# The batch loop of an adaLN attention and expert kernel, written over its 24 score units instead of over 16 steps

## The reference, cut to what matters

```python
h = _layernorm(x) * (1 + ca) + sa
Q, K, V = split_heads(h @ W_q.T), split_heads(h @ W_k.T), split_heads(h @ W_v.T)   # 16 heads of 2*8
A1 = causal(einsum(Q1, K1) * scaling);  A2 = causal(einsum(Q2, K2) * scaling)
O = (softmax(A1) - lam * softmax(A2)) @ V
O = O / sqrt(mean(O * O, -1) + EPS) * rms_scale * (1.0 - LAMBDA_INIT)
x = x + ga * (O @ W_o.T)
h = _layernorm(x) * (1 + cb) + sb
logits = h @ router_w.T + router_b          # top 2 of 8, softmax over the two
x = x + gb * sum over the two experts of gate * (silu(h @ gate_w.T) * (h @ up_w.T)) @ down_w.T
```

## Time and profile before

| | |
|---|---|
| median of 3 runs | 1679.91 us (1677.23 to 1682.1) |
| the profiled execution | 1678.91 us, span 1677.1 us |
| PE busy | 1340.8 us, 80% of the span |
| DVE busy | 1228.7 us, 73% |
| ACT busy, POOL busy | 859.4 us, 857.3 us, 51% each |
| mean granted clock of TensorE | 0.903 of 2.4 GHz |

### The profile page before, as it was taken

How to read it: one execution, slowest core, us unless ns; L and a number is a source line. 1 busy time by engine, 2 the same in 40 slices (tenths; PEclk the granted TensorE clock), 3 DMA queues, 4 the chain that set the end, 5 groups by cost and what they waited for, 6 DMA issues and landing times. The chain is left out here.

```text
span 1677.1 us, 44178 instructions
## 1 busy us (share of the span) xinstructions
PE 1340.8 (80%) x14048; PEld 940.4 (56%) x14049; DVE 1228.7 (73%) x3090; ACT 859.4 (51%) x1918; POOL 857.3 (51%) x1283
## 2 busy tenths in 40 slices
PE   1578888888888888888888888885199999999960
PEld 0345555555555555555555555553178888888850
DVE  3467887888888888888888888876756666666647
ACT  1156667666766676667666766664123333333320
POOL 0135566666666666666666666665323333333334
PEclk9999989998999899989998999896589999999985
DMA  5453444344434443444344434410111111111129
GB/s 203 99 111 76 112 109 101 86 111 109 105 85 108 112 105 84 111 111 105 83 111 111 106 83 108 105 39 17 43 44 44 44 44 46 43 44 45 44 76 296
DMA packets 182624, 151.73 MB, mean 90 GB/s; under 512 B 29555, under 2 KB 165369, under 8 KB 182068
## 3 DMA queue, kind: packets, MB, share of 16 engines
q1 hardware_dynamic: 165124, 122.11, 30.2%
q0 software_dynamic: 8448, 16.93, 3.3%
q10 hardware_dynamic: 8880, 10.49, 1.8%
HBM read 88.26 MB, written 60.51 MB: 89 GB/s over the span
## 5 line engine op out<-in xcount | busy, mean ns | idle before, releaser
L1190 DVE TENSOR_REDUCE mx<-p_max 128x2 f32<-128x512 f32 (+1 forms) x768 | 504.9, 685 | 198.3 <-PE p_max L816 188.9
L1009 ACT ACTIVATE probs<-p_exp 128x512 f32<-128x512 f32 x768 | 440.4, 601 | 239.7 <-PE p_exp L837 150.9
L1430 POOL TENSOR_SCALAR_AFFINE_SELECT probs<-probs 128x256 f32<-128x256 f32 (+1 forms) x768 | 366.3, 486 | 344.6 <-ACT probs L1009 333.3
L866 PE MATMUL p_out<-probs,v 128*32 128x256 f32 (+1 forms) x4096 | 253.3, 371 | 42.1 <-ACT ot L1000 35.7
L659 POOL DMA_INDIRECT pair_out<-on,v x136 | 133.7, 983 | 282.4 <-ACT on L569 274.6
L808 PE MATMUL p_max<-kt,qt 50*128 50x256 bf16 x1024 | 199.3, 293 | 35.6 <-ACT probs L1009 19.0
L866 PEld LDWEIGHTS p_out<-probs,v 128*32 128x32 f32 x4096 | 124.0, 119 | 145.2 <-POOL probs L1430 67.9
L837 PE MATMUL p_exp<-qt,kt 52*128 52x256 bf16 x1024 | 205.2, 289 | 0.0
L816 PE MATMUL p_max<-tri,ids 64*128 64x128 bf16 (+1 forms) x768 | 188.7, 253 | 0.0
L633 DVE TENSOR_TENSOR ot<-ot,p_max 128x512 f32<-128x512 f32 x136 | 93.5, 688 | 123.6 <-PE p_max L520 105.0
L816 PE MATMUL p_max<-tri,idb 64*128 64x128 bf16 (+1 forms) x768 | 172.3, 252 | 0.0
(11 more groups left out here) (174 smaller groups left out, 2750.5 us busy)
## 6 DMA issues: line engine op xcount, KB each, us to landing
qt<-q_parts SPq DMA_DIRECT2D x128, 192.0 KB
q_parts<-part_h SPq DMA_DIRECT2D x96, 128.0 KB, 1.9
kt<-k_parts SPq DMA_DIRECT2D x128, 96.0 KB
v<-rows_sorted SPq DMA_DIRECT2D x136, 65.0 KB, 1.8
q_parts<-part_m SPq DMA_DIRECT2D x64, 128.0 KB, 1.9
kt<-k_parts SPq DMA_DIRECT2D x128, 64.0 KB
qt<-pair_out SPq DMA_DIRECT2D x32, 256.0 KB, 5.0
mods<-mod_rows SPq DMA_DIRECT2D x32, 192.0 KB
```

The source lines that it names most:

```text
L866: m = nc.tensor.matmul(p_out[32 * j:32 * j + 32, pair, SEQ - n:SEQ], v[:, b.par, tile, 2 * g + head, :], src, start=(tile == 0), stop=(til ...
L1009: nc.scalar.activation(probs[:, quad % 2, k, :], p_exp[:, n % 3, :], ACT.Exp, scale=SCALE).then_inc(exp_done.sem, 1)
L1190: V.reduce_max(mx[:, w, tile, t, heads[0]:heads[-1] + 1], p_max[:, bank, :].rearrange("p (h k) -> p h k", h=len(heads)), AX.X, negate=True ...
L1430: G.affine_select(out=blocks, in_=blocks, compare_op=ALU.is_ge, fill=zero, base=0, pattern=[[0, count], [1, P]], channel_multiplier=-1).th ...
```

## The change

The loop `for s in range(16)` becomes `for u in range(24)` on PE, DVE, ACT and POOL. Each engine does one unit and then the extra work that the code names for that u. No product, reduce or copy is added or left out, and all sizes stay. What changes is after which unit each extra piece stands (units counted from 0; before, an even step s stands after unit s + s // 2, an odd one after the second of its two units, and a number with a star is a piece that DVE does between the two units of an odd step):

| piece | engine | after unit, before | now |
|---|---|---|---|
| `outputs` 6, 7 of bC | PE | 0, 3 | 0, 2 |
| `outputs` 0 to 5 of b2 | PE | 6, 9, 12, 15, 18, 21 | 6, 8, 12, 14, 18, 20 |
| `xn` transposes, `project` 0, `project` 1 | PE | 0, 2, 5 | 3, 4, 7 |
| `on_tok` transposes, `wo`, `h2` transposes | PE | 3, 5, 6 | 3, 5, 7 |
| `outputs_to_rows` of bC | PE | 8, 9 | 10, 11 |
| logits, V product, ranks | PE | 11, 12, 15 | 9, 13, 16 |
| `max_to_rows` of b2, of b1 | PE | 2, 14 | 1, 14 |
| `outputs_to_rows` of b2 | PE | 20, 21 | 17, 19 |
| `on_tok`, `xtmp` | DVE | 0, 6 | 1, 7 |
| `rest_part` 0, 1 | DVE | 3, 6 | 6, 9 |
| first statistics, their means | DVE | 7*, 9 | 2, 3 |
| `normalise` of bC | DVE | 9, 10* | 11, 13 |
| `minus_max` of b2, of b1 | DVE | 0, 12 | 0, 12 |
| top 8; indices and `topf`; `chosen`, `both` | DVE | 13*, 13*, 13* | 11, 14, 15 |
| second statistics, their means | DVE | 12, 13* | 15, 16 |
| sum of squares; ranks and carry; positions | DVE | 16*, 16*, 18 | 17, 18, 20 |
| `normalise` of b2 | DVE | 21, 22* | 19, 21 |
| `inverse_roots` 1 and 2, 3 and 4 | DVE | 21, 21 | 22, 23 |
| `copy_outputs` 3 of bC, 0 to 2 of b2 | ACT | 5, 11, 17, 23 | 3, 9, 15, 21 |
| `xn`, `h2` of the next turn's batches | ACT | 23 | 0, 1 of that turn |
| scatter of four row tiles (indirect DMA) | POOL | 18, 20, 21, 23 | 21, 22, 22, 23 |
| `o` = sum of two halves, `osq` = its square | POOL | 12, 14 | 14, 15 |

The two `outputs_to_rows` of bC also change banks, and the lists `MISC0` and `MISC1` with them. The diff, cut to its core:

```diff
-        MISC0 = [(ht_ready, 1, 2), (r_ready, 1, 2), (r_ready, 2, 2), (on2_ready, 4, -1),
+        MISC0 = [(ht_ready, 1, 2), (r_ready, 1, 2), (r_ready, 2, 2), (on2_ready, 3, -1),
                  (v_ready, 1, 1), (on2_ready, 1, 0)]
         MISC1 = [(nmt_ready, 2, 0), (ont_ready, 1, -2), (attn_scaled, 1, -2), (h2t_ready, 1, -3),
-                 (on2_ready, 3, -1), (route, 1, -3), (nmt_ready, 1, 1), (route, ROUTE_CARRY, -3),
+                 (route, 1, -3), (on2_ready, 4, -1), (nmt_ready, 1, 1), (route, ROUTE_CARRY, -3),
...
-                for s in range(NH):
-                    n = s + s // 2
-                    scores(b1, b2, n)
-                    if s % 2:
-                        scores(b1, b2, n + 1)
-                    if s % 2 == 0:
-                        g = s // 2 - 2
-                        if g >= 0 and active(b2):
-                            outputs(b2, g)
-                        if g < 0 and active(bC):
-                            outputs(bC, g + PAIRS)
-                    if s == 0 and active(bA):
-                        mix_free(pe, i, 0, 0)
-                        wait(pe, xn_ready, bA)
-                        for tile in range(NT):
-                            m = nc.tensor.transpose(p_mix[:, 0, tile * P:(tile + 1) * P], xn[:, tile, :], idf[:])
-                        m.then_inc(xt_ps.sem, 1)
...
+                    scores(b1, b2, u)
+                    if u in (0, 2) and active(bC):
+                        outputs(bC, PAIRS - 2 + u // 2)
+                    if u in (6, 8, 12, 14, 18, 20) and active(b2):
+                        outputs(b2, 2 * (u // 6 - 1) + u % 6 // 2)
+                    if u == 1 and active(b2):
                         max_to_rows(i, b2, 1, 0)
...
+                    if u == 3 and active(bA):
...
+                    if u == 4 and active(bA):
                         wait(pe, ht_ready, bA)
                         project(i, bA, 0, 1)
...
+                    if u == 5 and active(bW):
...
-                    if s == 3 and active(bA):
-                        project(i, bA, 1, 2)
-                    if s == 5 and active(bC):
-                        outputs_to_rows(i, bC, 1, 0, 1, 4)
-                    if s == 6 and active(bC):
-                        outputs_to_rows(i, bC, 1, 1, 0, 3)
-                    if s == 4 and active(bR):
+                    if u == 7 and active(bR):
                         mix_free(pe, i, 1, 3)
...
-                    if s == 7 and active(bR):
-                        mix_free(pe, i, 1, 5)
+                    if u == 7 and active(bA):
+                        project(i, bA, 1, 2)
+                    if u == 9 and active(bR):
+                        mix_free(pe, i, 1, 4)
                         wait(pe, h2t_ready, bR)
...
+                    if u == 10 and active(bC):
+                        outputs_to_rows(i, bC, 1, 0, 0, 3)
+                    if u == 11 and active(bC):
+                        outputs_to_rows(i, bC, 1, 1, 1, 5)
...
-                    if s == 9 and active(b1):
+                    if u == 14 and active(b1):
                         max_to_rows(i, b1, 0, 6)
-                    if s == 10 and active(bR):
+                    if u == 16 and active(bR):
 
...
-                    if s == 13 and active(b2):
+                    if u == 17 and active(b2):
                         outputs_to_rows(i, b2, 0, 0, 0, 5)
-                    if s == 14 and active(b2):
+                    if u == 19 and active(b2):
                         outputs_to_rows(i, b2, 0, 1, 1, 8)
 
...
-                    if s == 15 and (active(bL) or active(bW)):
-
...
+                    if u == 0 and (active(bA) or active(bR)):
+
+                        act.wait_ge(newton, NEWTON * (i.n + LEAD - 1))
+                    if u == 0 and active(bA):
...
+                    if u == 2 and active(bL):
+                        wait_half(dve, x_loaded[bL.par], bL)
...
+                    if u == 6 and active(bA):
                         rest_part(bA, 0)
-                    if s == 4 and active(bW):
+                    if u == 7 and active(bW):
...
-                    if s == 4 and active(bA):
+                    if u == 9 and active(bA):
                         rest_part(bA, 1)
...
+                    if u == 10 and active(bR):
+
...
+                    if u == 11:
                         for k in range(2):
                             if active(bC):
...
-                    if s == 7 and active(bC):
...
+                    if u == 12 and active(b1):
+                        minus_max(b1, 0, 0)
...
+                    if u == 13 and active(bC):
                         for k in range(2):
-                            normalise(bC, 1, 1, 0, k)
...
-                            V.tensor_tensor(lg[:], p_mix[:, 1, 0:NT * NE].rearrange("p (t e) -> p t e", t=NT),
-                                            rb[:].unsqueeze(1).to_broadcast([P, NT, NE]), ALU.add).then_inc(route.sem, 1)
-                        if active(bW):
-                            wait(dve, x1_ready, bW)
-                            settle(dve)
...
+                    if u == 14:
                         if active(bR):
                             wait(dve, route, bR, ROUTE_TOP)
...
+                    if u == 15:
+                        if active(bR):
                             wait(dve, route, bR, 6)
                             V.tensor_tensor(chosen[:], iota8[:].unsqueeze(1).to_broadcast([P, 2 * NT, NE]),
                                             topf[:].rearrange("p j t -> p (j t)").unsqueeze(2).to_broadcast([P, 2 * NT, NE]),
                                             ALU.is_equal).then_inc(route.sem, 1)
+                        if active(bW):
+                            wait(dve, x1_ready, bW)
+                            settle(dve)
+                            statistics(bW, 1, stats2)
+                        if active(bR):
                             wait(dve, route, bR, 7)
                             V.tensor_tensor(both[:], chosen[:, 0:NT, :], chosen[:, NT:2 * NT, :], ALU.add).then_inc(route.sem, 1)
-                    if s == 11 and active(bC):
+                    if u == 16 and active(bW):
+                        for tile in range(NT):
+                            mean_and_variance(bW, 1, stats2, tile)
+                    if u == 17 and active(bC):
                         wait(dve, osq_ready, bC)
                         V.reduce_sum(rms_ss[:], osq[:], AX.X).then_inc(rms_sum.sem, 1)
-                    if s == 11:
+                    if u == 18:
...
-                    if s == 14:
-                        if active(b2):
-                            for k in range(2):
-                                normalise(b2, 0, 0, 0, k)
-                        inverse_roots(i, [1, 2, 3, 4])
...
+                    if u == 22:
+                        inverse_roots(i, [1, 2])
+                    if u == 23:
+                        inverse_roots(i, [3, 4])
...
-                    if s in (12, 13, 14, 15) and active(bR):
-
-                        k = s - 12
+                    for k in {21: (0,), 22: (1, 2), 23: (3,)}.get(u, ()):
```

More of the change, by code:

```diff
@@ L1095, in body @@
-                    if s == 15 and active(bW):
-                        if not (bW.static and bW.c < 2):
-                            wait_half(act, scattered[bW.par], bW.plus(-2))
-                        wait(act, h2t_ps, bW.plus(-2))
-                        wait(act, h2_copied, bW.plus(-2))
-                        settle(act)
-                        for tile in range(NT):
-                            c = NT * NH + NT + tile
-                            nc.scalar.activation(h2[:, bW.par, 0, tile, 0:DIM], xres[:, bass.ds(bW.n * SEQ + tile * DIM, DIM)],
-                                                 ACT.Identity, bias=neg_mr[:, NT + tile:NT + tile + 1],
-                                                 scale=rstd[:, c:c + 1]).then_inc(xn2_ready.sem, 1)
@@ L1439, in body @@
                 bA, b2, bC, bW, bR = (i.plus(d) for d in (2, 0, -1, -2, -3))
-                for s in range(NH):
+                for u in range(NBANKS):
                     if active(b2):
-                        mask_bank(b2, s + s // 2)
-                        if s % 2:
-                            mask_bank(b2, s + s // 2 + 1)
-                    if s == 5 and active(bW):
-                        wait(pool, attn_scaled, bW)
-                        xb = xres[:, bass.ds(bW.n * SEQ, SEQ)]
-                        G.tensor_tensor(xb, xb, xtmp[:].rearrange("p t c -> p (t c)"), ALU.add).then_inc(x1_ready.sem, 1)
-                    if s in (4, 6) and active(bA):
-                        low_part(bA, (s - 4) // 2)
-                    if s == 0 and active(bR):
+                        mask_bank(b2, u)
+                    if u == 2 and active(bR):
                         wait(pool, xn2_ready, bR)
@@ L1459, in body @@
```

(8 more changed lines are left out.)

182 lines of the change are left out of this document (92 added, 90 removed).

## The result

The changed kernel takes **1837.85 us** (median of 4 runs, 1831.29 to 1842.33), the kernel before 1681.01 in the same session (4 runs, 1677.23 to 1684.34): a ratio of **1.093, interval 1.089 to 1.098**, 9.3% slower. The forecast was 1722, its range ended at 1775. The direction was right, the size a quarter of what came. The profiled execution takes 1831.29 us (span 1829.5), 152.4 more than that of before.

A forecast was written before the change was run, and what follows sets the result against it. PE was taken to bound units 0 to 7 and DVE the rest. Larger parts 31.7 plus waits gave 33.6, plus clock 1.4 made 35.0 us a turn against 33.6: 1722 us over 31 turns, range 1645 to 1775.

The forecast's parts named there:

- the sum of the larger parts: Over seven ranges of units, the larger of PE's and DVE's work adds up to 31.7 us a turn.
- the waits and the walk: Per-range work of 31.7 plus waits of 1.1, 0.5 and 0.3: 33.6 us a turn, against 32.0 for the old turn.
- the price of the clock: Cost of PE's clock falling at units 15 and 16 and slowing 17 to 20: 1.4 us a turn, 1.6 before.
- `xtmp`: PE's h2 transposes behind unit 7 wait for DVE's xtmp, with nothing covering it: 1.1 us a turn.
- `both`: PE idles 2.4 us after unit 16, before the ranks, waiting for DVE's both; it was 1.12.
- `ht`: PE's project 0 waits for ACT's ht with only unit 4 between: 0.5 us a turn.
- `rest_part` 1: PE's outputs_to_rows of bC waits for it at unit 10: 0.2 us a turn.
- The rival of the free POOL: DVE's minus_max, topf and chosen no longer blocked by POOL: 32.8 us a turn, 1654 us; chance of faster 0.28.
- The three savings in the rival's sum: DVE's minus_max, topf and chosen save 1.1, 0.4 and 0.7 us, 2.2 in all, where DVE bounds the turn.
- What the other moves bring lies under cover.: Other moves, such as earlier copy_outputs and POOL's scatters, change nothing because DVE's list is full in those units.
- the clock as one fall per turn: A fall at units 15 and 16 costs from nothing to 3.3 us a turn; 1.4 was taken.
- The lead-in at nothing: Lead-in and tail cost nothing, having the same turns and chain; any one edit there would show some 3 us.

The follow-up runs named there:

- early_split: The changed kernel with the chain that makes Q's and K's parts moved back to about where it stood before: 1766.29 us, ratio 1.052.
- es_route: early_split with DVE's indices and topf after unit 12, chosen after 13 and both after 14: 1797.09 us, ratio 1.073.
- late_low: The kernel before with only POOL's second low_part moved from after unit 9 to after unit 12: 1713.89 us, ratio 1.019.
- split_saves: The changed kernel with SP's Q saves waiting for low_part 0 alone and only the K saves for low_part 1: 1797.35 us, ratio 1.071.
- load_first: The changed kernel with SP's loads for unit 0 issued ahead of move_max instead of behind it: 1806.45 us, ratio 1.077.
- es_xtmp: early_split with DVE's xtmp after unit 6 instead of after unit 7: 1736.22 us, ratio 1.032.

## Why the prediction was right and wrong

**Right in the main: the sum of the larger parts.** PE sets the pace of some units and DVE of others, and the change moved work so that both lists are full at different places. early_split, in which the loop is nearly idle (12.5 us of weight loads' waits for `kt` between 200 and 1200 us), has turns of 35.21 and 36.47 us in a row, mean 35.74; the forecast was 35.0. In its terms: the waits and the walk were to add 1.6 us a turn (33.6 against 32.0), and PE's idle time grew by 2.3; the price of the clock was to fall by 0.2 (1.4 against 1.6), and PE's busy time fell by 0.15. That the sum holds range by range of units was not measured. (Its seven larger parts add up to 31.6, not 31.7.)

**Right: `xtmp`.** Forecast 1.1 us a turn, in the trace 1.1 (29.0 us over 26), and by the chip 30 and 31 us for moving it. **Right: `both`.** Forecast 2.4, measured 2.43, longest 2.4 over 26 turns, and the clock falls behind it. **Right in kind, small in size:** `ht`, forecast 0.5, 0.31 here and 0.62 a turn earlier, 9.9 us over 20; `rest_part` 1, forecast 0.2, 0.41 here. DVE idles 1.83 before unit 8, forecast 1.5 or more, then 0.53.

**The rival of the free POOL is out.** From DVE's timeline, to set against the earlier trace rows:

```profile
605.59 0.46 DVE L1194 TENSOR_SCALAR nm<-mx,ones_col 128x32 bf16<-128x32 f32 x1
...
609.32 0.67 DVE L1339 TENSOR_SCALAR topf<-top8i,ones_col 128x4 f32<-128x4 uint32 x1
...
610.50 0.87 DVE L1344 TENSOR_TENSOR chosen<-iota,topf 128x32 f32<-128x32 f32 x1
```

`nm`'s pieces (the second takes 1.11), `topf` and `chosen` are still stretched, and beside them POOL has `part_l` (605.98 + 1.16), `o` and `osq` (610.29 + 1.03). So it is in every middle turn: 0.46 + 1.10, 0.67 and 0.87 us where the kernel before had 0.61 + 1.22, 1.03 and 0.35, together 0.1 less. DVE's busy time did not change (774.6 us over the 28 turns, 774.3 before). The three savings in the rival's sum (1.1, 0.4 and 0.7) are not what the kernel before shows; its own shortest times give 1.4, 0.8 and 0.2, 2.4 in all for 2.2. es_route, where all three did come free, was not faster either, but with the wait for K grown beside it that is no clean test.

**Wrong: "What the other moves bring lies under cover."** This is the step that failed. I followed each moved step to the next engine that reads it in the same turn, and stopped at POOL's `low_part`. Its reader is SP, and there stand nine saves, four transfers of `move_max`, eight loads and unit 0 of the next turn. The whole queue was costed at nothing because it was not followed at all; the earlier trace rows could not show it, since a DMA that is in time leaves no wait. In the kernel before, the last loads of K for unit 0 and unit 0 itself read so (timelines of SP and of PE):

```profile
614.10 1.14 SPq L761 DMA_DIRECT2D kt<-k_parts  x3
```

```profile
620.99 0.21 PE L811 MATMUL p_max<-kt,qt 50*128 50x128 bf16 x1 [1.14 <-issue]
```

From the last issue (615.24) to unit 0 are 5.75 us. With the 4.8 that the loads of the changed kernel needed, 1.0 us was to spare in this turn (by the medians above, 18.0 - 15.3 = 2.7). `low_part` 1 moved by three units, and that spare time was gone. In place of nothing, PE waits 42.8 us for `kt` between 200 and 1200 us. Shown: late_low (+34 us for one such step), early_split (-72), split_saves and load_first (-40 and -31).

**Wrong: the clock as one fall per turn.** I bounded it by one fall, 3.3 us. In stretches of 0.5 us, the granted clock falls below 0.75 of 2.4 GHz 29 times over the 28 turns of the kernel before and of early_split, and 44 times in the changed one. With the wait for K there are two holes, and PE can meet units 0 to 7, which PE bounds, at half clock: 11.93 us for 0 to 7 at 0.74, where the earlier trace rows has 10.77 at 1.00. Of the 4.14 us a turn, 2.00 are what early_split gives back and 2.14 what it leaves; by PE's busy time all of the 2.00 is clock (61.4 us over 28 turns, 2.19 each, with idle time up by 0.19). What the wait would cost at an unchanged clock the runs don't show, since every edit that takes the wait away also changes when the clock falls.

**Wrong: the lead-in at nothing.** It is +20.0 us, a unit's shift of the row included. `p_max`'s wait for `kt` before the first `on_tok` went from 25.3 us over 4 to 38.3 over 4, so 13 us stand with the loop, which has little other work beside it while few batches are in flight. es_xtmp still has +13.6 (first `on_tok` at 165.50).

**Open.** What holds DVE and ACT at unit 1 when the loads go ahead of `move_max` in the early kernels, and with it what of load_first's own shortfall is clock alone.

## What to carry to other kernels

When a step moves, follow its result until it comes back to where the turn began, through saves, every entry of the DMA queue and loads, and compare that loop's length with the turn, even where the trace of before shows no wait at all. In such a queue look at what stands ahead of the load that matters: here the saves of Q and `move_max`, each worth 30 to 40 us when it was taken out of the way of K in the changed kernel. Expect that removing one of two holes gives back less than its length, or shifts the hole, and judge by the turn and its granted clock, not by the wait that vanished.

## What the hardware showed that I had not expected

`on_tok` (two SBUF inputs on DVE, 512 wide) takes 0.69 us at the median in the kernel before and 0.87 in the changed one, 1.39 at most. Where it begins under a mask of POOL, it ends 0.55 us after that mask does (626.51 + 1.11, the masks 625.85 + 1.22). POOL's indirect DMAs (about 1.0 us each) stand near it too, but beside one of them alone it took 0.68 at 1266.56. So it looks like the blocking seen at `minus_max`; it was not tried by itself. Turn lengths go by the granted clock more than by the waits named in the trace: in load_first 35.46 us at 0.95, and 39.01 and 39.19 at 0.80 and 0.81 with the same instructions and the same order, and PE idle for 7.3 us in the short turn and 5.7 and 6.5 in the long ones.
